# A graph layer on one core: keys, context and token mixing moved from the first stage and the prologue into the edge loop

## The chip, the cores and the metric

The kernel runs on one core of a Trainium2 chip. The metric is the time of one execution on the device in microseconds (us). The engines are PE (TensorE matmul, with PEld for its weight loads), DVE (VectorE), ACT (ScalarE), POOL (GpSimd) and SP (SyncE, which here only issues DMAs). Each has a program of its own; they meet at semaphores only.

## The reference, cut to what matters

There are N = 3125 nodes of D = 256 features (25 blocks of 128 rows, the last one short) and E = 50000 edges, sorted by destination.

```
xn = layernorm(x)
# graph attention: 4 heads of 64 features
h  = einsum('ni,hio->hno', xn, W)
e  = leaky(attn_src[:, src] + attn_dst[:, dst], 0.2) * edge_weight
p  = exp(e - max(e));  alpha = p / (segment_sum(p, dst)[dst] + 1e-10)
g  = segment_sum(h[:, src] * alpha, dst)               # per head, concatenated: 256
# linear attention over all nodes: 4 heads of 32
q, k, v = split(xn @ W_qkv);  k = softmax(k over the nodes)
context[h] = k[h].T @ v[h];   mix = (q * 32**-0.5 @ context) @ W_out + b_out
x1 = x + g + mix
# feed-forward on the better half of the tokens, 256 -> 1024 -> 256
xn2 = layernorm(x1);  w = xn2 @ wr + br
out = x1 + xn2 + (where a token ranks in the top 1561: w * (gelu(xn2 @ w1 + b1) @ w2 + b2))
```

The maximum over all edges is not known in advance: the kernel keeps a running maximum over the groups and rescales what it has accumulated.

## The kernel before, in words

All engines' programs are written out by hand; the order of the work on each engine is the order of its lines, and a `wait_ge` on a semaphore is all that couples them. There is no planner.

**First stage, blocks t = 0 to 24.** DVE takes mean and variance (L745, L787) and normalizes (`normed`, L757) into a ring of five blocks; PE transposes the block (L432); ACT copies the transposed block out of PSUM (L615); `project` on PE multiplies it by `wbig` (L417: h for 256 features, the source and destination logits, and v, 392 columns together) and by `wqk` (L423: k and q, transposed). DVE copies h out (L764, a row of the table `htab`, which SP stores with L285) and v (L765); ACT copies k and q (L604). POOL adds the output bias to x (L365). Under t = 0 DVE also makes the tables of destination indices (L806 to L828), which SP stores and reloads before the first row of `htab` goes out (L269 to L280). POOL makes the table `iotab` of block numbers at t = 20 (L363). SP loads the tokens x at the start, between the weights; the late weights (L306 to L312) and the lists of the first eight edge groups go out between the row stores.

**Prologue.** When the last row of `htab` is in memory POOL starts to gather. Meanwhile ACT exponentiates k (L623); PE transposes it (L519) and sums the context over 25 blocks (L523); DVE takes the four diagonal parts out; PE multiplies by W_out (L529); and 25 products of q with that matrix (L534) are added to x by DVE (L1034). `expand`, `turn` and `logits` for the first groups run in between.

**Edge loop, 98 groups of 512 edges.** Groups 0 to 7 are written out, groups 8 to 87 are ten passes of a hardware loop whose body holds eight groups, and 88 to 97 are written out again (`groups`, L207). For group g:
- SP loads its lists (L296 to L303); POOL gathers 4 tiles of 128 rows of `htab` by source (L383) into a ring of four groups; it may start group g + 4 when the messages of g are made.
- DVE (`step`, L1036): messages of g (L936, rows times exponentials), one-hot of g (L998), running maximum with group g + 1 (`group_max`, L930, one partition), addition of the sums of g - 1 to the accumulators (`add_last`, L941), logits of g + 2 (L911 to L923), one-hot columns of g + 3 (L870). On every second group its registers with the block numbers are loaded.
- PE (`step`, L537): the sums of g, eight matmuls of 260 columns (L483), and after the first two of them the maximum for g + 1 spread over 128 partitions (`spread`, L479); then the edge maxima of g + 2 transposed (`turn`, L472), and the destination logits of g + 3 (`expand`, L452, L460).
- ACT (`step`, L660): waits for the spread maximum, copies it twice (L666, L667), two exponentials of the logits (L671, L672), in split groups the sums of g - 1 under two masks (L658), then the rescale factors (L645, L648).

Each group's edges end in one block of nodes or in two; 24 groups are such split ones and take the branches.

**After the loop**: normalization, the second layernorm, the feed-forward over 25 blocks (L564, L577), ranks of the tokens by counting (L1126 to L1132) and the output. The change leaves it as it is but for the names of its buffers.

Of the kernel before, what the change touches and what calls it, by code (L numbers as in the profile page):

```python
# [6 lines left out]
P = 128  # L7
# [4 lines left out]
ALU = mybir.AluOpType  # L12
# [7 lines left out]
TILES = 4  # L20
RING = 4
LISTS = 8
BODY = 5


def gps_layer(nc, x_in, src_in, dst_in, ew_in, gw_in, gas_in, gad_in, wqkv_in, wout_in, bout_in,
# [25 lines left out]
    ADV = HEADS + QK  # L52
    HW = ROW + ADV
# [8 lines left out]
    LOOPS = NG // LISTS  # L62
    KSEL = max(1, int(0.5 * N))
    KK = KSEL - 1 if KSEL > 1 else 1
    assert EREST % TILES == 0 and D == HF == 256 and NB % BODY == 0 and QK == P

# [5 lines left out]
    w_d = nc.dram_tensor("w_d", (NB, P), F32, kind="Internal").ap()  # L72

    with ExitStack() as ctx:
# [10 lines left out]
        kq = sb("kq", [P, 2, NB * P])  # L85
        adv = sb("adv", [P, NB, ADV])
        wbig = sb("wbig", [P, KC, HW])
        wqk = sb("wqk", [P, KC, 2 * QK])
# [16 lines left out]
        xnT = sb("xnT", [P, BODY, KC, P])  # L105
# [35 lines left out]
        rg = sb("rg", [1, 2])  # L141
        rj = sb("rj", [1, P])
        Rsb = sb("Rsb", [P, 2])
        negR = sb("negR", [P, 2])
        Rlast = sb("Rlast", [P, NB])
# [5 lines left out]
        ksums = sb("ksums", [P, NB // BODY])  # L151
        kmaxs = sb("kmaxs", [P, NB // BODY])
        ekt = sb("ekt", [P, BODY, P])
# [13 lines left out]
        wrow = kq[:, 0, :]  # L167
        junk = kq[:, 1, :]
# [6 lines left out]
        for name in ("constants_ready y_weighted gelu_table masks_ready k_padding_zero wqkv_loaded "  # L175
                     "block_iota_ready kmax_of_batch sp_go gp_go dve_go act_go deviation_ready b_out_loaded "
                     "w_loaded late_weights_loaded a_loaded w_times_a w_a_ready stats_ready mean_var_ready "
                     "rstd_ready xn_ready xn_turned xnT_ready h_projected rows_staged attn_dst_v_taken "
                     "kq_projected kq_taken b_out_added dst_loaded table_steps tables_stored ranges_loaded "
                     "last_dst_loaded padding_loaded attn_dst_split kmax_steps k_exp ksum_steps ek_turned "  # L180
                     "ek_taken context_summed context_taken c2_multiplied c2_taken mix_multiplied mix_added "
                     "edge_max logit_sum logit_leaky logit_weighted max_turned running_max max_spread "
                     "max_copied exp_ready messages_ready columns_last columns_block attn_dst_last "
# [16 lines left out]
        FIRST_BATCHES = ((0, 1), (1, BODY - 1))  # L200
        TURN_BANKS, MIX_BANKS = (3, 4, 6), (3, 4, 6)
        WT_AT = 6
        DLP = 12

        block = ctx.enter_context(nc.Block())

# [959 lines left out]
```

## Time and profile before

| what | value |
|---|---|
| runs (3) | 829.38, 820.99, 830.68 us; median 829.38 us |
| profiled execution | 831.26 us, its span 829.2 us |
| mean granted TensorE clock | 0.841 of 2.4 GHz |
| busy share of the span | PE 84%, PEld 65%, DVE 72%, ACT 30%, POOL 56% |
| DMA | 82.60 MB, mean 100 GB/s |

The span runs from the first to the last instruction of the core. Busy shares count executing instructions; register, branch, semaphore and DMA-issuing instructions count as idle. POOL's gathers (DMA_INDIRECT) count as busy while POOL prepares them; the transfer itself runs on the DMA engines. An idle time is put down to the engine whose semaphore came last, or to "issue" where the profile shows nothing that was waited for. A matmul's duration runs to the modelled end of its result, so consecutive ones overlap: the distance of their starts is the rate.

### The profile page before, as it was taken

To read this page: it belongs to the slowest core of one execution; us is meant where nothing else is said; L and a number is where in the kernel's file an instruction comes from. 1 tells how busy PE (TensorE), PEld (TensorE's weight loads), DVE (VectorE), ACT (ScalarE), POOL (GpSimd) and SP (SyncE) were. 2 spreads that over 40 slices of the span, in tenths; PEclk is the share of its full clock that TensorE was granted. 3 is DMA by queue.
4 is the path that set the end of the run, shared out by engine and by line. 5 is a ranking of instruction groups with operands and counts; after the bars stand their busy time and mean duration, and the time that the engine had idled before them with its cause. 6 is when DMAs were issued, how large, how long until landed. Compare 5 with 4: busy or idle time off the path is not lost.

```text
span 829.2 us, 18805 instructions
## 1 busy us (share of the span) xinstructions
PE 698.8 (84%) x4369; PEld 537.4 (65%) x4370; DVE 594.7 (72%) x1631; ACT 247.1 (30%) x1013; POOL 466.6 (56%) x512
## 2 busy tenths in 40 slices
PE   3799689877878788879888888789867989999995
PEld 2577566654555565656565656566647879999994
DVE  7665267765767676766676767677769982989895
ACT  1222502222322223322232323233333422333331
POOL 5233437777777777777776777777701260333332
PEclk9999786887887878876586968787878999999998
DMA  6255415655655555655555656566400002000000
GB/s 209 58 184 79 93 53 126 142 137 133 138 131 135 134 135 136 141 128 129 129 133 125 134 135 136 126 137 138 107 21 1 1 2 80 26 33 28 26 26 22
DMA packets 104814, 82.60 MB, mean 100 GB/s; under 512 B 67133, under 2 KB 91566, under 8 KB 104561
## 3 DMA queue, kind: packets, MB, share of 16 engines
q0 software_dynamic: 18816, 52.21, 24.4%
q1 hardware_dynamic: 85873, 29.16, 16.6%
q14 instruction: 100, 0.82, 0.3%
q8 instruction: 25, 0.41, 0.2%
HBM read 74.47 MB, written 6.84 MB: 98 GB/s over the span
## 4 chain that ended last, share of the span: by engine, by line
PE 44%; issue 18%; DVE 18%; DVEq 6%; DMA 4%; ACT 3%; POOL 3%; SPq 2%; ACTq 2%; POOLq 0%
PE ps L483 17%; PE ps L564 8%; PE ps L577 8%; DVE oh L998 4%; PE ps L417 3%; POOL G L383 3%; DVEq L231 3%; PE ps L479 3%; DMA G<-htab,srcr 2%; DVE msg L936 2%; PE ps L423 2%; DVE wprod L1094 1%; DMA x<-in_x 1%; DVE G L1077 1%; ACTq L231 1%
## 5 line engine op out<-in xcount | busy, mean ns | idle before, releaser
L383 POOL DMA_INDIRECT G<-htab,srcr x392 | 372.2, 949 | 158.3 <-issue 133.5
L483 PE MATMUL ps<-msg,oh 128*128 128x260 f32 x784 | 298.6, 518 | 73.8 <-DVE oh L998 73.2
L483 PEld LDWEIGHTS ps<-msg,oh 128*128 128x128 f32 x784 | 174.1, 245 | 103.9 <-issue 78.5
L936 DVE TENSOR_TENSOR msg<-G,ps 128x1024 f32<-128x1024 f32 x98 | 119.2, 1216 | 45.1 <-issue 29.6
L564 PEld LDWEIGHTS ps<-xnT,w 128*128 128x128 f32 x800 | 98.0, 201 | 3.8 <-issue 1.8
L564 PE MATMUL ps<-xnT,w 128*128 128x128 f32 x800 | 98.5, 284 | 2.1 <-ACT wide L727 1.6
L666 ACT ACTIVATE negR<-ps 128x1 f32<-128x1 f32 x98 | 16.8, 171 | 257.8 <-PE ps L479 244.0
L577 PE MATMUL ps<-w,wide 128*128 128x256 f32 x400 | 90.4, 380 | 1.2 <-DVE acc L1101 1.2
L998 DVE TENSOR_TENSOR oh<-ps,dmr 128x512 f32<-128x512 f32 x98 | 67.3, 687 | 21.2 <-issue 19.9
L577 PEld LDWEIGHTS ps<-w,wide 128*128 128x128 f32 x400 | 74.3, 190 | 10.4 <-issue 1.4
L396 POOL TENSOR_SCALAR G<-acc,mw 128x256 f32<-128x256 f32 x25 | 23.1, 923 | 99.4 <-DVE mw L1134 90.2
L452 PE MATMUL ps<-ad,ohT 128*128 x1464 | 72.5, 175 | 5.1 <-DVE ohT L870 1.7
L452 PEld LDWEIGHTS ps<-ad,ohT 128*128 128x128 bf16 x1464 | 63.1, 118 | 9.9 <-issue 6.3
L479 PEld LDWEIGHTS ps<-rg,ones 1*128 1x128 f32 x196 | 34.7, 220 | 41.2 <-issue 41.1
L727 ACT ACTIVATE wide<-ps,b 128x128 f32<-128x128 f32 x200 | 54.2, 389 | 3.5 <-PE ps L564 3.4
L389 POOL TENSOR_TENSOR x<-x,acc 128x256 f32<-128x256 f32 x25 | 22.0, 885 | 54.5 <-DVE acc L1087 54.5
L1129 DVE TENSOR_SCALAR_CACHE_REDUCE kq<-kq,wtok 128x3125 f32<-128x3125 f32 (+24 forms) x25 | 46.6, 1866 | 0.0
L1126 DVE TENSOR_SCALAR_CACHE_REDUCE kq<-kq,wtok 128x128 f32<-128x128 f32 (+23 forms) x24 | 44.9, 1871 | 0.0
L870 DVE TENSOR_SCALAR ohT<-dstb,nodeid 128x512 bf16<-128x512 uint16 x98 | 38.6, 393 | 8.7 <-issue 7.4
L941 DVE SCALAR_TENSOR_TENSOR acc<-acc,fsc,ps 128x260 f32 x74 | 35.2, 475 | 13.2 <-issue 10.3
L417 PE MATMUL ps<-wbig,xnT 128*128 128x392 f32 x100 | 40.1, 526 | 4.3 <-DVE adv L765 4.2
L479 PE MATMUL ps<-rg,ones 1*128 1x1 f32 x196 | 43.1, 287 | 0.0
(139 smaller groups left out, 805.5 us busy)
## 6 DMA issues: line engine op xcount, KB each, us to landing
dstb<-dstu_d SPq DMA_DIRECT2D x98, 128.0 KB
G<-htab,srcr POOLq DMA_INDIRECT x392
htab<-hst SPq DMA_DIRECT2D x25, 130.0 KB, 2.6
out<-G SPq DMA_DIRECT2D x24, 128.0 KB, 1.7
x<-in_x SPq DMA_DIRECT2D x4, 640.0 KB, 8.5
w<-in_L_ffn_w SPq DMA_DIRECT2D x4, 512.0 KB
kq<-w_d SPq DMA_DIRECT2D x1, 1600.0 KB, 6.3
dmr<-dstm_d SPq DMA_DIRECT2D x98, 2.0 KB
```

The costliest lines, as they stand in the source:

```text
L383: gp.indirect_dma_start(G[:, q % RING, k, :], None, htab, bass.IndirectOffsetOnAxis(ap=srcr[:, q, k:k + 1], axis=0)).then_inc(s_g[q % RING ...
L417: m = pe.matmul(ps[:, 2 + b, 0:HW], xnT[:, t % BODY, kc, :], wbig[:, kc, :], start=(kc == 0), stop=(kc == KC - 1))
L452: m = pe.matmul(ps[:, p, 4 * k:4 * k + 4], ohT[:, columns, k:GE:TILES], ad3[:, bass.ds(b, 1), j, :].rearrange("p a h -> p (a h)"), start=F ...
L479: pe.matmul(ps[:, 5, 0:1], ones[:, :], rg[:, q % 2:q % 2 + 1], start=True, stop=True).then_inc(S["max_spread"], 1)
L483: m = pe.matmul(ps[:, 3 + p, 0:ROW], oh[:, p, k, :], msg[:, p, k, :], start=(k == 0), stop=(k == TILES - 1))
L564: m = pe.matmul(ps[:, 2 + half, (c % 4) * P:(c % 4 + 1) * P], w1[:, kc, c * P:(c + 1) * P], xnT[:, t % BODY, kc, :], start=(kc == 0), stop ...
L577: m = pe.matmul(ps[:, 4 + t % 3, 0:D], hT[:, t % 2, c, :], w2[:, c, :], start=(c == 0), stop=(c == FC - 1))
L727: m = act.activation(hT[:, t % 2, c, :], ps[:, 2 + half, (c % 4) * P:(c % 4 + 1) * P], ACT.Gelu_apprx_tanh, bias=b1[:, c:c + 1])
L936: dve.tensor_tensor(msg[:, p, :, 0:HF].rearrange("p k (h o) -> p k h o", h=HEADS), G[:, q % RING, :, 0:HF].rearrange("p k (h o) -> p k h o ...
L998: dve.tensor_tensor(oh[:, q % 2, :, :], iotap.unsqueeze(1).to_broadcast([P, TILES, P]), dmr[:, q, :].unsqueeze(2).to_broadcast([P, TILES, ...
L1126: dve.tensor_scalar(junk[:, 0:lo], wrow[:, 0:lo], wt, 0.0, ALU.is_ge, ALU.add, accum_out=cnt[:, t, 0:1]).then_inc(S["counted"], 1)
L1129: dve.tensor_scalar(junk[:, lo:N], wrow[:, lo:N], wt, 0.0, ALU.is_gt, ALU.add, accum_out=cnt[:, t, 1:2]).then_inc(S["counted"], 1)
```

## The change

- The first stage projects h and the two attention logits only (264 columns); `evacuate_h` moves from DVE to ACT. The transposed blocks `xnT` of all 25 blocks are kept, instead of a ring of five.
- Block 0 is loaded, normalized and projected by itself. The other token loads, and b_out's, move from SP's queue to ACT's, ahead of ACT's first activation. The index tables are stored after row store 6 instead of before the first. Three edge lists go out among the last row stores, five after them, then the late weights. POOL zeroes acc block by block behind the bias addition, instead of in one piece at the start.
- Keys: PE makes k for 512 nodes at a time (`keys`, seven chunks, two of them ahead of the first `expand`); DVE takes them out together with their maximum.
- The running maximum: `turn` becomes a product of the edge maxima, broadcast over 128 columns, with the identity, so that DVE's `group_max` leaves the negated maximum on all 128 partitions. `spread`, its place inside the sums, and ACT's two copies go.
- The ten passes of the loop are split in five and five. In the first five, each of the five groups in SLOTS takes one node block: ACT stages the transposed block and the exponential of its keys (`stage_keys`), PE makes v and the transposed keys (`make_pair`, at the end of its step) and adds the pair of the slot before to the context; ACT takes the pair out of PSUM in the following group, after that group's exponentials and before its rescaling. Between the halves the context, W_out and the transposed W_q are multiplied into one 256x256 matrix M (`take_context`, `multiply_context`). In the last five passes PE multiplies a staged block by M (`mix`) and DVE adds the product to x in the following group (`add_mix`).

```diff
+SLOTS = (0, 2, 3, 5, 6)
...
-    HW = ROW + ADV
+    HW = ROW + HEADS
...
+        def looped(eng, lo, hi, step, side=None):
+
+            with eng.Fori(lo, hi):
+                for q in range(LISTS):
+                    step(None, q, side)
...
+                    if t == TABLES_AT:
+                        store_tables()
+                    if t == TABLES_AT + 7:
+                        spread_tables()
+                    if t == TABLES_AT + 10:
+                        sp.wait_ge(S["tables_stored"], 80)
+                    if t in LISTS_AT:
+                        step(LISTS_AT.index(t), LISTS_AT.index(t))
+                unrolled(step, range(len(LISTS_AT), LISTS))
+                for tile, array in loads:
+                    sp.dma_start(tile, array).then_inc(S["late_weights_loaded"], 16)
+                looped(sp, 1, LOOPS - 1, step)
+                unrolled(step, TAIL)
...
+                gp.memset(acc[:, t, :], 0.0).then_inc(S["acc_zeroed"], 1)
...
-                if t >= 2:
-                    pe.wait_ge(S["kq_taken"], t - 1)
-                for c in range(2):
-                    for kc in range(KC):
-                        m = pe.matmul(ps[:, 4 + b, c * P:(c + 1) * P], wqk[:, kc, (1 - c) * P:(2 - c) * P], xnT[:, t % BODY, kc, :],
-                                      start=(kc == 0), stop=(kc == KC - 1))
-                m.then_inc(S["kq_projected"], 1)
...
+            def keys(c):
+
+                lo = 4 * c
+                if c == 0:
+                    pe.wait_ge(S["wqkv_loaded"], 32)
+                if c >= 2:
+                    pe.wait_ge(S["k_taken"], c - 1)
+                wide = min(WIDE, N - c * WIDE)
+                for kc in range(KC):
+                    nodes = xnT[:, lo:lo + 4, kc, :] if wide == WIDE else xnT[:, lo, kc, 0:wide]
+                    m = pe.matmul(ps[:, 5 + c % 2, 0:wide], wqkv[:, kc, QK:2 * QK], nodes, start=(kc == 0), stop=(kc == KC - 1))
+                m.then_inc(S["k_projected"], 1)
 
...
-                pe.transpose(ps[0:1, 2, 0:P], rm[:, q % 2:q % 2 + 1], ident[:, :]).then_inc(S["max_turned"], 1)
-
-            def spread(q, ready):
-
-                pe.wait_ge(S["running_max"], ready)
-                if ready is n:
-                    pe.wait_ge(S["exp_ready"], n)
-                pe.matmul(ps[:, 5, 0:1], ones[:, :], rg[:, q % 2:q % 2 + 1], start=True, stop=True).then_inc(S["max_spread"], 1)
-
-            def add_messages(p, tiles=range(TILES)):
...
+            def add_context(s, last=False):
+                return pe.matmul(ps[:, 6, 0:P], pair[:, s, 0:P], pair[:, s, P:2 * P], start=False, stop=last, skip_group_check=True)
+
+            def make_pair(q):
+
+                if q in SLOTS:
+                    pe.wait_ge(S["pair_taken"], passed)
+                    pe.wait_ge(S["block_staged"], passed)
+                    pe.sem_inc(S["pe_go"], 1)
+                    add_context((SLOTS.index(q) - 1) % BODY)
+                    for kc in range(KC):
+                        pe.matmul(ps[:, 5, 0:P], xs[:, kc, :], wqkv[:, kc, 2 * QK:3 * QK], start=(kc == 0), stop=(kc == KC - 1))
+                    pe.transpose(ps[:, 5, P:2 * P], es[:, :], ident[:, :]).then_inc(S["pair_made"], 1)
+                    pe.reg_add(passed, passed, 1)
+
+            def multiply_context():
+                pe.wait_ge(S["pair_taken"], NB + 1)
+                add_context(BODY - 1, True).then_inc(S["context_summed"], 1)
+                pe.wait_ge(S["context_taken"], MIX_HEADS)
+                pe.wait_ge(S["late_weights_loaded"], 16 * 9)
+                pe.matmul(ps[:, 6, 0:D], ctxT[:, :], wout[:, :], start=True, stop=True).then_inc(S["c2_multiplied"], 1)
+                pe.wait_ge(S["c2_taken"], 1)
+                for kc in range(KC):
+                    m = pe.matmul(ps[:, 5, kc * D:(kc + 1) * D], wqT[:, kc, :], C2[:, :], start=True, stop=True)
+                m.then_inc(S["m_multiplied"], 1)
+                pe.wait_ge(S["m_taken"], 1)
+
+            def mix(q):
+                if q in SLOTS:
+                    pe.wait_ge(S["mix_added"], passed)
+                    pe.wait_ge(S["block_staged"], passed)
+                    pe.sem_inc(S["pe_go"], 1)
+                    for kc in range(KC):
+                        m = pe.matmul(ps[:, 5, 0:D], xs[:, kc, :], M[:, kc, :], start=(kc == 0), stop=(kc == KC - 1))
+                    m.then_inc(S["mix_multiplied"], 1)
+                    pe.reg_add(passed, passed, 1)
+
+            def step(g, q, side=None):
+                sums(q)
                 if q % 2 == 1 and (g is None or g + 3 < NG):
                     load_ranges(pe, regs, cursor, (q + 3) % LISTS)
                 if g is None or g + 2 < NG:
                     turn(q + 2, n)
                 if g is None or g + 3 < NG:
                     expand((q + 3) % LISTS, n)
...
+            unrolled(step, FIRST)
+            pe.wait_ge(S["query_taken"], 1)
+            looped(pe, 1, 1 + TURNS, step, make_pair)
+            multiply_context()
+            looped(pe, 1 + TURNS, LOOPS - 1, step, mix)
+            pe.wait_ge(S["mix_added"], 2 * NB + 1)
...
+            for i, (base, blocks) in enumerate(NORMED[1:]):
+                if i < len(NORMED) - 2:
+                    act.dma_start(x[:, base:base + blocks, :], x_in[base * P:(base + blocks) * P, :].rearrange("(b p) c -> p b c", p=P)).then_inc(s_x[1 + i], 16)
+                else:
+                    act.dma_start(x[:, base:NB - 1, :], x_in[base * P:(NB - 1) * P, :].rearrange("(b p) c -> p b c", p=P)).then_inc(s_x[1 + i], 16)
+                    act.wait_ge(S["constants_ready"], 1)
+                    act.dma_start(x[0:REST, NB - 1, :], x_in[(NB - 1) * P:N, :]).then_inc(s_x[1 + i], 16)
+                if i == 0:
+                    act.wait_ge(S["constants_ready"], 8)
+                    act.activation(negR[:, 0:1], eps[:, 0:1], ACT.Sqrt)
+            act.dma_start(boutb[:, :], bout_in.rearrange("(a d) -> a d", a=1).to_broadcast([P, D])).then_inc(S["b_out_loaded"], 16)
...
+            def evacuate_h(t):
+
+                act.wait_ge(S["h_projected"], t + 1)
+                if t >= BODY:
+                    act.wait_ge(s_tab[t % BODY], 16 * (t // BODY))
+                act.activation(hst[:, t % BODY, :], ps[:, 2 + t % 2, 0:ROW], ACT.Copy).then_inc(S["rows_staged"], 1)
+                act.activation(adst[:, t, :], ps[:, 2 + t % 2, ROW:HW], ACT.Copy).then_inc(S["attn_dst_taken"], 1)
...
+            def stage_tokens(done):
+                act.activation(xs[:, :, :], xnT[:, bass.ds(act.snap(u, min_val=0, max_val=NB - 1), 1), :, :].rearrange("p a c n -> p (a c) n"), ACT.Copy).then_inc(S[done], 1)
+
+            def stage_keys(q):
+
+                if q - 1 in SLOTS:
+                    act.wait_ge(S["pair_made"], made)
+                    act.activation(pair[:, SLOTS.index(q - 1), :], ps[:, 5, 0:2 * P], ACT.Copy).then_inc(S["pair_taken"], 1)
+                    act.reg_add(made, made, 1)
+                if q in SLOTS:
+                    stage_tokens("tokens_staged")
+                    t = act.snap(u, min_val=0, max_val=NB - 1)
+                    act.activation(es[:, :], kT[:, bass.ds(t * P, P)], ACT.Exp, bias=kmax[:, 1:2], accum_out=ksums[:, bass.ds(t, 1)]).then_inc(S["block_staged"], 1)
+                    act.reg_add(u, u, 1)
+
+            def stage_block(q):
+
+                if q in SLOTS:
+                    act.wait_ge(S["mix_multiplied"], made)
+                    act.sem_inc(S["act_go"], 1)
+                    stage_tokens("block_staged")
+                    act.reg_add(u, u, 1)
+                    act.reg_add(made, made, 1)
+
...
+            def step(g, q, side=None):
                 p = q % 2
                 if q % 2 == 0:
                     load_ranges(act, regs, cursor, q)
                 first, start, last = blocks_of(act, regs, q)
-                act.wait_ge(S["max_spread"], n)
-                act.activation(negR[:, p:p + 1], ps[:, 5, 0:1], ACT.Copy, scale=-1.0).then_inc(S["max_copied"], 1)
-                act.activation(Rsb[:, p:p + 1], ps[:, 5, 0:1], ACT.Copy).then_inc(S["max_copied"], 1)
+                act.wait_ge(S["running_max"], n3)
                 act.wait_ge(S["summed_last"], n3)
-                act.wait_ge(S["max_copied"], copies)
                 e = et[:, p, 0:16].rearrange("p (k h) -> p k h", k=TILES)
                 act.activation(msg[:, p, :, HF:ROW], e, ACT.Exp, bias=negR[:, p:p + 1])
                 act.activation(exq[:, p, :, :], e, ACT.Exp, bias=negR[:, p:p + 1]).then_inc(S["exp_ready"], 1)
+                if side:
+                    side(q)
                 act.wait_ge(S["added_last"], n)
                 act.wait_ge(S["max_kept_last"], n)
...
+                before = -LOWEST if ready == 3 else negR[:, (q + 1) % 2:(q + 1) % 2 + 1]
+                dve.tensor_scalar(rj[:, :], ps[:, 2, 0:P], -1.0, before, ALU.mult, ALU.min, accum_out=negR[:, q % 2:q % 2 + 1]).then_inc(S["running_max"], 1)
...
+            for c in range(CHUNKS):
+                lo, hi = c * WIDE, min((c + 1) * WIDE, N)
+                dve.wait_ge(S["k_projected"], c + 1)
...
+            def take_context():
+                dve.wait_ge(S["block_staged"], NB)
+                dve.tensor_reduce(ksum[:, 0:1], ksums[:, :], AX.X, ALU.add).then_inc(S["ksum_steps"], 1)
+                dve.wait_ge(S["ksum_steps"], 1)
+                dve.reciprocal(ksum[:, 1:2], ksum[:, 0:1]).then_inc(S["ksum_steps"], 1)
+                dve.wait_ge(S["context_summed"], 1)
+                for h in range(MIX_HEADS):
+                    s = slice(h * DIM_HEAD, (h + 1) * DIM_HEAD)
+                    dve.tensor_copy(ctxT[s, s], ps[s, 6, s]).then_inc(S["context_taken"], 1)
+                dve.wait_ge(S["c2_multiplied"], 1)
+                dve.wait_ge(S["ksum_steps"], 2)
+                dve.tensor_scalar(C2[:, :], ps[:, 6, 0:D], ksum[:, 1:2], float(DIM_HEAD) ** -0.5, ALU.mult, ALU.mult).then_inc(S["c2_taken"], 1)
+
+            def add_mix(q):
+                if q - 1 in SLOTS:
+                    t = dve.snap(u, min_val=0, max_val=NB - 1)
+                    a = x[:, bass.ds(t, 1), :].rearrange("p a c -> p (a c)")
+                    dve.wait_ge(S["mix_multiplied"], mixed)
+                    dve.sem_inc(S["dve_go"], 1)
+                    dve.tensor_tensor(a, ps[:, 5, 0:D], a, ALU.add).then_inc(S["mix_added"], 1)
+                    dve.reg_add(u, u, 1)
+                    dve.reg_add(mixed, mixed, 1)
+
...
+                if side:
+                    side(q)
```

## Rows read from the trace of the kernel before

**Rows 1.** The chain that ended last, from the page: shares of the span by engine.

```profile
PE 44%; issue 18%; DVE 18%; DVEq 6%; DMA 4%; ACT 3%; POOL 3%; SPq 2%; ACTq 2%; POOLq 0%
```

**Rows 2.** Stretches: length, busy us (x instructions) per engine, clock, DMA share, GB/s.

```profile
50.00:100.00 50.00, 42.02 (x255) 33.45 (x254) 23.08 (x66) 17.88 (x53) 18.64 (x17) 0.90 0.45 93
...
200.00:300.00 100.00, 82.78 (x511) 56.64 (x510) 69.03 (x197) 26.89 (x129) 75.17 (x79) 0.78 0.59 135
```

**Rows 3.** Groups by line: xcount | busy, mean ns | idle before, releasers.

```profile
L383 POOL DMA_INDIRECT G<-htab,srcr x392 | 372.2, 949 | 158.3 <-issue 133.5 <-DVE msg L936 24.8
...
L936 DVE TENSOR_TENSOR msg<-G,ps 128x1024 f32<-128x1024 f32 x98 | 119.2, 1216 | 45.1 <-issue 29.6 <-ACT ps L672 15.0
```

**Rows 4.** Lines L383 and L936: ns min/median/max, first and last start us.

```profile
L383 POOL DMA_INDIRECT G<-htab,srcr x392: 940/946/1194, 92.5 to 602.1; - x196
...
L936 DVE TENSOR_TENSOR msg<-G,ps x98: 1201/1221/1223, 123.1 to 613.1; 128x1024 f32<-128x1024 f32 x98
```

**Rows 5.** DVE timeline (start us, us, instruction, [idle, releaser]): messages opening groups 8 to 88.

```profile
159.90 1.22 DVE L936 TENSOR_TENSOR msg<-G,ps 128x1024 f32<-128x1024 f32 x1 [0.17 <-ACT ps L672]
...
202.76 1.22 DVE L936 TENSOR_TENSOR msg<-G,ps 128x1024 f32<-128x1024 f32 x1 [3.60 <-issue]
...
230.24 1.21 DVE L936 TENSOR_TENSOR msg<-G,ps 128x1024 f32<-128x1024 f32 x1
...
234.20 1.21 DVE L936 TENSOR_TENSOR msg<-G,ps 128x1024 f32<-128x1024 f32 x1
...
569.40 1.22 DVE L936 TENSOR_TENSOR msg<-G,ps 128x1024 f32<-128x1024 f32 x1
```

**Rows 6.** Timeline of POOL: the seventeenth gather.

```profile
125.13 0.94 POOL L383 DMA_INDIRECT G<-htab,srcr  x1 [12.75 <-DVE msg L936]
```

**Rows 7.** Timeline of one block of the first stage, PE.

```profile
78.74 0.38 PE L432 MATMUL ps<-ident,xn 128*128 128x128 f32 x2
...
78.96 1.48 PE L417 MATMUL ps<-wbig,xnT 128*128 128x392 f32 x4
...
80.28 1.05 PE L423 MATMUL ps<-xnT,wqk 128*128 128x128 f32 x8
```

**Rows 8.** Groups by line and shape: xcount | busy, mean ns | idle before.

```profile
L1034 DVE TENSOR_TENSOR x<-ps,x 128x256 f32<-128x256 f32 x25 | 10.6, 425 | 3.9 <-PE ps L534 3.8
...
L604 ACT ACTIVATE kq<-ps 128x256 f32<-128x256 f32 x25 | 9.6, 383 | 47.2 <-PE ps L423 47.2
```

**Rows 9.** Timeline around POOL's table of block numbers.

```profile
60.38 5.54 POOL L363 TENSOR_TENSOR wide<-iota,blkbase 128x3200 f32<-128x3200 f32 x1
61.58 4.48 DVE L757 TENSOR_SCALAR xn<-x,mv,rstd 128x256 f32<-128x256 f32 x1
...
67.10 0.72 POOL L365 TENSOR_TENSOR x<-x,boutb 128x256 f32<-128x256 f32 x1 [0.23 <-DVE xn L757]
```

**Rows 10.** Timeline of the start: two token loads; PE's restart.

```profile
9.86 3.63 SPq L246 DMA_DIRECT2D x<-in_x  x2
...
26.11 2.95 PE L417 MATMUL ps<-wbig,xnT 128*128 128x392 f32 x4 [4.17 <-DVE adv L765]
```

**Rows 11.** Timeline of the prologue: DVE's first one-hot columns.

```profile
91.19 0.35 DVE L870 TENSOR_SCALAR ohT<-dstb,nodeid 128x512 bf16<-128x512 uint16 x1 [4.16 <-issue]
```

**Rows 12.** Timeline of a group in the loop, PE at full clock.

```profile
460.52 0.68 PE L483 MATMUL ps<-msg,oh 128*128 128x260 f32 x2 [0.62 <-DVE oh L998]
...
461.43 1.58 PE L483 MATMUL ps<-msg,oh 128*128 128x260 f32 x6
...
462.08 0.26 ACT L672 ACTIVATE ps<-et,negR 128x16 f32<-128x16 f32 x1
...
463.27 0.20 ACT L648 ACTIVATE Rlast<-Rsb 128x1 f32 x1
...
463.29 0.73 PE L452 MATMUL ps<-ad,ohT 128*128 x12
```

**Rows 13.** Timeline of a group in the loop, PE at half clock: its last six sums.

```profile
410.28 2.97 PE L483 MATMUL ps<-msg,oh 128*128 128x260 f32 x6
```

More of the change, by code:

```diff
@@ L72, in gps_layer @@
     w_d = nc.dram_tensor("w_d", (NB, P), F32, kind="Internal").ap()
+    NORMED = ((0, 1), (1, BODY - 1)) + tuple((lo, BODY) for lo in range(BODY, NB, BODY))
     with ExitStack() as ctx:
@@ L200, in gps_layer, with unrolled @@
         FIRST_BATCHES = ((0, 1), (1, BODY - 1))
[L201 removed]
         WT_AT = 6
         DLP = 12
+        TABLES_AT, LISTS_AT = 6, (17, 19, 21)
         block = ctx.enter_context(nc.Block())
[L207 to L218 removed]
+        FIRST, TAIL = range(LISTS), range((LOOPS - 1) * LISTS, NG)
+        def looped(eng, lo, hi, step, side=None):
+            with eng.Fori(lo, hi):
+                for q in range(LISTS):
+                    step(None, q, side)
+        def unrolled(step, which):
+            for g in which:
+                step(g, g % LISTS)
         numbers = iter(range(1000))
@@ L436, in _ @@
             project(NB - 1)
+            keys(0)
+            keys(1)
             pe.wait_ge(S["ranges_loaded"], 32)
@@ L524, in _ @@
-            spread(0, 3)
+            expand(1, 2)
+            for c in range(2, CHUNKS):
+                keys(c)
+            pe.wait_ge(S["k_taken"], CHUNKS)
+            for kc in range(KC):
+                m = pe.transpose(ps[:, 5, kc * P:(kc + 1) * P], wqkv[:, kc, 0:QK], ident[:, :])
+            m.then_inc(S["query_turned"], 1)
+            pe.matmul(ps[:, 6, 0:P], zrow[:, 0:P], zrow[:, 0:P], start=True, stop=False, skip_group_check=True)
+            turn(0, 2)
             turn(1, 3)
@@ L535, in _ @@
-            pe.wait_ge(S["mix_added"], NB)
-            def step(g, q):
-                sums(q, lambda: spread(q + 1, n) if g is None or g + 1 < NG else None)
+            def add_context(s, last=False):
[10 more added lines that the diff above has]
+                    pe.reg_add(passed, passed, 1)
@@ L691, in step @@
                 rescale(fsc, p, last, "factor_last", n5, "max_kept_last")
-                for r, by in ((n, 1), (n3, 1), (n5, 1), (copies, 2)):
-                    act.reg_add(r, r, by)
+                for r in (n, n3, n5):
+                    act.reg_add(r, r, 1)
             act.wait_ge(S["masks_ready"], 2)
             act.wait_ge(S["iota_taken"], 1)
-            groups(step)(act)
+            unrolled(step, FIRST)
+            act.wait_ge(S["kmax_steps"], 2)
+            act.wait_ge(S["k_padding_set"], 1)
+            looped(act, 1, 1 + TURNS, step, stage_keys)
+            act.wait_ge(S["m_multiplied"], 1)
+            act.activation(M[:, :, :], ps[:, 5, 0:KC * D].rearrange("p (c n) -> p c n", c=KC), ACT.Copy).then_inc(S["m_taken"], 1)
+            act.reg_mov(u, 0)
+            act.reg_mov(made, 1)
+            looped(act, 1 + TURNS, LOOPS - 1, step, stage_block)
+            unrolled(step, TAIL)
             act.wait_ge(S["added_last"], n)
@@ L778, in _ @@
             m.then_inc(S["w_a_ready"], 1)
-            invert(0, BODY, 1)
-            for t in range(BODY):
+            invert(1, BODY - 1, 2)
+            for t in range(1, BODY):
                 normed(t).then_inc(S["xn_ready"], 1)
@@ L1037, in step @@
+            def step(g, q, side=None):
                 add, leak, weight, reduce = [lambda: None] * 4
```

300 lines of the change are left out of this document (110 added, 190 removed).

## The prediction

> **What bounds the kernel now.** I read the chain of waits first, then the stretches, then the two groups that recur in every edge group, then the order of time. The chain [rows 1] names PE for 44% and DVE for 18%, but that averages over stages. The stretches [rows 2] separate them: in 50 to 100 us (mostly projection) PE has 42.0 of 50 us; in the edge loop (200 to 300) PE has 82.8, POOL 75.2 and DVE 69.0 of 100, at a granted clock of 0.78, so PE moves between its two levels. No engine is full there, so the rate has to be read from the groups.
>
> The groups give it [rows 3]: 392 gathers of 949 ns with 133.5 us of "issue" idle between them, about 0.3 each, are 1.25 us apiece, 5.0 per edge group, 40.0 for a pass of eight. DVE's messages multiply runs once per group, from 123.1 to 613.1 [rows 4], so its starts are the clock of the loop: 159.90 (group 8) to 569.40 (group 88) [rows 5] are ten passes in 409.5 us, 40.95 each. But POOL also waited 24.8 us for DVE's messages [rows 3], 12.75 of it at once, with all four ring slots full while DVE was still in the prologue [rows 6]; later, too, DVE is now and then the late one. So **two limits lie within 1 us of each other**: POOL at 40.0, and the chain of DVE, PE and ACT. What lengthens that chain costs in full; shortening it gains at most 0.95 us a pass.
>
> Once per pass DVE also sits 3.6 us ahead of its messages with no releaser but "issue" [rows 5]; ten such idles make 29.6 us [rows 3]. They come at the loop's jump back; the change keeps the number of passes, so they stay. What follows the last messages (613.1 to 829.2, 216 us) it leaves alone.
>
> **The change, part by part.** *Projection.* A block's PE work is 0.22 us of transposes, then 1.32 of four 392-column matmuls (78.96 to 80.28), then eight products for k and q in 1.05, of which the next block overlaps 0.17 [rows 7]: 2.42 with no gap. The eight go; 392 columns become 264, so 1.32 becomes 0.89, and PE needs 1.1. ACT takes over the copies out of PSUM: 0.38 for a 256-column one [rows 8], two such and a short one, about 1.0. POOL's bias addition takes 0.72 and alternates with DVE's normalization 0.23 apart where pressed [rows 9], 0.95; POOL now also zeroes a block of acc each time, which I put at 0.3, between nothing and another 0.72, since it reads nothing. So 1.3 us a block, bounds 1.1 and 1.7.
>
> Here a row speaks against the change: beside POOL's 5.54 us table of block numbers one normalization took 4.48 us [rows 9]. PE at 2.42 a block hid that; at 1.3 I charge 3 us of it. The Trainium skill (SBUF — State Buffer, section "SBUF: two separate sides") says that DVE and GpSimd share a port pair under an exclusive lock, the loser blocking for the whole instruction. The trace agrees with that; taken strictly, the zeroing would cost its full length in every block.
>
> The start: PE restarted at 26.11, after DVE's index tables and copies, with two blocks done [rows 10]. Afterwards five normalized blocks are ahead of the tables and DVE no longer copies, so five are done by then. But the token loads move to ACT's queue; SP spent 3.63 us issuing two of them [rows 10], and ACT's first square root stands behind all of its issues, to about 11 us. That moves the restart to 27.5 (bounds 26 and 31). Then 20.5 blocks by 1.3, plus 3: the projection ends near 57. On SP's queue the table stores move behind row store 6, four issues and a wait that held back every row until now; the first three edge lists stand between the last row stores and cost about a microsecond. The late weights move behind the lists; their first use is after the fifth pass, which hides them.
>
> *Prologue.* Register loads held DVE 4.16 us before its first one-hot [rows 11]; that stays, with about 2 us of splitting ahead of it and 3 of two expansions behind. New on the path are seven key chunks, each four 512-column matmuls: by the 392-column row 1.7 us at full clock, twice that after an idle stretch; five lie behind the expansions, 10 us. Their copies on DVE run beside the next chunk; without that cover they would add about 0.8 each. Logits, maximum and exponential: 5. First messages near 81, **42 us earlier** (36 to 47). The context chain and the 25 mixing products leave this stretch. The gathers start near 61 instead of 92.5 [rows 4] and fill the ring by 81, so the 12.75 us stall goes.
>
> *Every group.* The `spread` matmul leaves PE (it holds the third sum to 461.43, 0.91 after the first) [rows 12] and two copies leave ACT; the maximum becomes a two-pass product, +0.1. DVE's wait for ACT's exponential goes: 15.0 us over 98 groups [rows 3], 1.2 per eight.
>
> *First five passes: keys and context.* PE gets, five times a pass, seven products of 128 columns: by the row of eight [rows 7] 0.95 at full clock, 1.6 to 1.9 at half. A PE step at full clock ends 3.5 us after its first sum (460.52 to 464.02) [rows 12]; without the spread and with the second pass 3.05, so a pair is ready 4.15 after its group's sums begin. **The price is a new wait on ACT:** one step later ACT waits for that pair before it rescales, and the exponential of the group after that is queued behind. From the pair on: copy 0.38 [rows 8]; rescale 0.8 (1.1 from 462.34 to 463.47 [rows 12], partly overlapped); on even groups a register load, 1.75 (two cost DVE 4.16, so under 2.1); exponentials 0.4: 3.3. Where the next block is staged, 0.8 more. DVE starts its messages 2 us before PE's sums and needs 3.96 a step (230.24 to 234.20) [rows 5], 4.5 with a register load, so it is ready for group 2 at 6.5, and the exponential comes at 4.15 + 3.3 = 7.45: 1.0 late. The same working gives 2.0 at group 4 (staging and load), 0.9 at group 7, nothing elsewhere: 3.9. A pass: 40.95 − 1.2 + 3.9 = 43.7. At half clock six sums take 2.97 instead of 1.58 [rows 12, 13] and the pair comes about 2.5 later; I put 0.3 a pass on that: **44.0**.
>
> *Last five passes: mixing.* DVE adds 0.43 [rows 8] and a wait, five times: 2.5. PE's four 256-column products take about 1.0, and only behind neighbouring slots does ACT still come late, 0.75. 40.95 − 1.2 + 3.25 = **43.0**. Between the halves the fused matrix makes four hops over PE, DVE and ACT with a PSUM copy on each: 4 us.
>
> *Sum*, on the profiled span of 829.2: −42 (head), −1.2 (first eight groups), 5 · 3.05 + 5 · 2.05 = +25.5 (passes), +4 (between), −1.5 (last ten groups): −15.2, **814**. The execution itself took 831.3, 2.1 more than its span; the median of the runs is 829.4, equal to the span, so 814 stands for the median too.
>
> **The rivals.** *A. Forecast, 814, chance 0.42.* The head gains 42 and the passes give back over half. On its own terms 802 to 828.
>
> *B. The passes stay with POOL.* If ACT's wait falls into slack, the gathers set the rate: they start 31.5 earlier, lose no 12.5, and 3 us of later stalls go: 829.2 − 47 = 782. For it: 1.25 us a gather, and ACT busy for 27 of 100 us [rows 2]. Against: POOL was already waiting for DVE. Chance 0.2.
>
> *C. Slower: PE at its half level becomes the bound of the passes.* A half-clock step is 3.05 + 1.9 = 4.95, plus 1.6 in five of eight: 48 a pass. The head's gain is spent when a pass reaches 45.0; 2% slower needs 46.7. At 48.3: 829.2 − 40.7 + 73 − 4 = 857. For it: clock 0.78 with PE at 83% [rows 2], and PE's net work a pass grows by 3 us (full) to 6 (half). Against: 0.90 where PE was packed [rows 2]. Chance 0.18.
>
> *D. PE rises to 2.4 GHz in the passes.* With fewer gaps the clock goes to 1.0 and the half-clock part of the 40.95, about 1.2, falls away: passes of 42.5 and 42.0, so 829.2 − 40.7 + 13 = 802. The Trainium skill (TensorE: Matmul & The Clock Gate, Part 1) states that idleness throttles the array and activity releases it; by that rule the added products partly pay for themselves. [rows 2] lean that way, 0.90 against 0.78, but the two stretches differ in more than that. Chance 0.2.
>
> **How the numbers follow.** The likeliest is 814. The range 780 to 846 takes in B at the low end, the head's bounds and passes up to 47; the outer part of C is left out. A measurement of this kernel can tell about 2% from no change, 812.8 to 846.0. Faster: B, most of D, a third of A, 0.48; slower: most of C and a corner of A, 0.15; same: 0.37.
>
> **What would show it.** Right: first messages near 81; gathers from 61 with no stall at the fifth group; in passes one to five the messages of groups 2, 4 and 7 waiting for ACT's exponential; 44 and 43 us a pass, and POOL waiting for messages in more groups than now. B would show passes of 40.0 and DVE waiting for G, C a clock below 0.75 and PE without idle, D a clock above 0.9. The forecast fails at its root if the projection stays above 1.7 us a block, for then the head gives less than 30, or if ACT never waits for the pair.

## The result, and the profile after

The changed kernel takes **834.8 us** (833.8 to 837.6 over 4 runs), the kernel before 829.2: a ratio of 1.0086, with a 95% interval of 1.0043 to 1.0128. It is slightly slower, where 814 and faster had been forecast. The profiled span went from 829.2 to 831.8.

The first view is again the line of DVE's messages, which open every edge group, beside that of the gathers, by groups (busy, mean ns | idle before, releasers).

```profile
L389 POOL DMA_INDIRECT G<-htab,srcr x392 | 373.1, 952 | 171.8 <-issue 122.8 <-DVE msg L985 48.9
L985 DVE TENSOR_TENSOR msg<-G,ps 128x1024 f32<-128x1024 f32 x98 | 119.0, 1214 | 73.4 <-ACT ps L726 52.1 <-issue 20.9
```

The messages' line by itself (ns min/median/max, first and last start):

```profile
L985 DVE TENSOR_TENSOR msg<-G,ps x98: 1200/1217/1223, 92.2 to 617.9; 128x1024 f32<-128x1024 f32 x98
```

Against [rows 3, 4]: the first messages come 30.9 us earlier (92.2, was 123.1), the last 4.8 later. DVE's wait for ACT's exponential (L726) went from 15.0 to 52.1 us, and POOL's wait for messages doubled, 24.8 to 48.9. Some 9 us of the 52.1 stand where "issue" stood before (29.6, now 20.9); all idle time ahead of the messages rose from 45.1 to 73.4. So the loop is longer, and DVE waits for ACT more, POOL for DVE. Cut by the starts of groups 0, 8, 48, 88 and 97 (us; "rest" is the span less the last start):

| profile | first messages | first 8 groups | passes 1-5 | passes 6-10 | groups 88 to 97 | rest | span |
|---|---|---|---|---|---|---|---|
| before | 123.1 | 36.8 | 203.7 | 205.8 | 43.7 | 216.1 | 829.2 |
| after | 92.2 | 36.8 | 234.8 | 215.7 | 38.4 | 213.9 | 831.8 |
| predicted difference | -42 | -1.2 | +15.2 | +14.3 | -1.5 | 0 | -15.2 |
| measured difference | -30.9 | -0.1 | +31.2 | +9.9 | -5.3 | -2.2 | +2.6 |

(The 4 us between the halves are put to passes 6 to 10 in the prediction's row; in the trace they fall into pass 5, which took 51.4.)

*The wait in the passes.* Pass 3, timelines of ACT, DVE and PE (start, us, instruction, [idle, releaser]): group 24's messages, sums and pair, the sums of group 25, the messages, sums and pair of group 26, and the messages of group 28.

```profile
219.89 1.22 DVE L985 TENSOR_TENSOR msg<-G,ps 128x1024 f32<-128x1024 f32 x1 [3.60 <-issue]
...
223.34 3.38 PE L490 MATMUL ps<-msg,oh 128*128 128x260 f32 x8 [5.59 <-DVE oh L1047]
...
228.15 0.27 PE L536 MATMUL ps<-ident,es 128*128 128x128 f32 x1
228.26 1.92 PE L490 MATMUL ps<-msg,oh 128*128 128x260 f32 x8
...
228.46 0.38 ACT L700 ACTIVATE pair<-ps 128x256 f32<-128x256 f32 x1 [4.49 <-PE ps L536]
229.47 0.29 ACT L678 ACTIVATE fsc<-negRlast,negR 128x1 f32 x1 [0.63 <-issue]
229.88 0.20 ACT L681 ACTIVATE negRlast<-negR 128x1 f32 x1
231.73 0.31 ACT L725 ACTIVATE msg<-et,negR 128x16 f32<-128x16 f32 x1 [1.64 <-issue]
231.94 0.26 ACT L726 ACTIVATE ps<-et,negR 128x16 f32<-128x16 f32 x1
...
232.23 1.22 DVE L985 TENSOR_TENSOR msg<-G,ps 128x1024 f32<-128x1024 f32 x1 [2.20 <-ACT ps L726]
...
234.20 3.81 PE L490 MATMUL ps<-msg,oh 128*128 128x260 f32 x8 [2.80 <-DVE oh L1047]
...
240.08 0.27 PE L536 MATMUL ps<-ident,es 128*128 128x128 f32 x1
240.39 0.38 ACT L700 ACTIVATE pair<-ps 128x256 f32<-128x256 f32 x1 [5.56 <-PE ps L536]
...
244.18 1.22 DVE L985 TENSOR_TENSOR msg<-G,ps 128x1024 f32<-128x1024 f32 x1 [3.33 <-ACT ps L726]
```

ACT sits idle 4.49 us until PE has turned the staged keys (L536); then come the copy, the rescaling, a register load (the 1.64 of "issue") and the exponential, and DVE's messages for group 26 are 2.20 late, for group 28 3.33. PE waits for DVE in its turn. The sums of group 24 follow 5.59 us of idle, most of it DVE's stop at the loop's jump back (group 24's messages, at 219.89, stand behind 3.60 us of "issue", as once a pass in the kernel before [rows 5]); they take 3.38 us at a granted clock of 0.56, where the sums of group 25 take 1.92 at 1.00. The late messages of group 26 then leave PE idle for 2.80 us, and its sums take 3.81 us at 0.50, the lower of the two levels.

*The head.* ACT's queue at the start; then ACT's and SP's when the stage is under way.

```profile
3.53 2.68 ACTq L633 DMA_DIRECT2D x<-in_x  x1
6.25 4.79 ACTq L635 DMA_DIRECT2D x<-in_x  x1
11.07 6.85 ACTq L639 DMA_DIRECT2D boutb<-in_L_mix_b_out  x1
17.97 0.29 ACT L643 ACTIVATE sd<-mv,eps 128x1 f32<-128x1 f32 x1 [15.22 <-issue]
...
33.25 0.44 PE L445 MATMUL ps<-ident,xn 128*128 128x128 f32 x2 [2.70 <-DVE xn L823]
...
45.04 1.06 PE L424 MATMUL ps<-wbig,xnT 128*128 128x264 f32 x4
45.93 0.38 PE L445 MATMUL ps<-ident,xn 128*128 128x128 f32 x2
46.15 1.06 PE L424 MATMUL ps<-wbig,xnT 128*128 128x264 f32 x4
...
44.93 0.39 SPq L269 DMA_DIRECT2D dstm_d<-wide  x1
45.37 9.26 SPq L283 DMA_DIRECT2D htab<-hst  x7
...
53.09 0.39 ACT L650 ACTIVATE hst<-ps 128x260 f32<-128x260 f32 x1 [4.01 <-DMA htab<-hst]
```

Three issues hold ACT for 14.3 us, so its first square root runs at 17.97 and PE restarts at 33.25 (26.11 before [rows 10]). A block then takes 1.11 us (45.04 to 46.15; 2.42 before [rows 7]), until ACT waits 4.01 us for the row stores that queue behind the index tables.

### The profile page after: what moved, and what is told of

It is laid out like the page before. It is cut to its first block, busy times and chain, and to the rows that moved or that the text cites. A ratio compares the mean times of both kernels' runs of the same rounds, so it can differ in the third digit from the quotient of the medians.

```text
span 831.8 us, 18655 instructions
## 1 busy us (share of the span) xinstructions
PE 653.5 (79%) x4258; PEld 541.0 (65%) x4259; DVE 574.4 (69%) x1591; ACT 253.8 (31%) x936; POOL 469.0 (56%) x537
## 4 chain that ended last, share of the span: by engine, by line
PE 42%; issue 20%; DVE 16%; ACTq 6%; DVEq 5%; ACT 5%; DMA 3%; POOL 2%; SPq 0%; POOLq 0%
PE ps L490 14%; PE ps L596 8%; PE ps L609 7%; DVE oh L1047 3%; PE ps L465 3%; ACTq L239 2%; POOL G L389 2%; PE ps L424 2%; DVEq L239 2%; PE ps L486 2%; PE ps L557 2%; DVE wprod L1164 1%; DMA G<-htab,srcr 1%; DVE stats L811 1%; DVE G L1147 1%
## 5 line engine op out<-in xcount | busy, mean ns | idle before, releaser
L490 PE MATMUL ps<-msg,oh 128*128 128x260 f32 x784 | 250.0, 474 | 98.7 <-DVE oh L1047 98.2
L985 DVE TENSOR_TENSOR msg<-G,ps 128x1024 f32<-128x1024 f32 x98 | 119.0, 1214 | 73.4 <-ACT ps L726 52.1
L465 PE MATMUL ps<-ad,ohT 128*128 x1464 | 77.4, 176 | 3.0 <-DVE ohT L919 2.0
L465 PEld LDWEIGHTS ps<-ad,ohT 128*128 128x128 bf16 x1464 | 67.3, 118 | 9.5 <-issue 3.4
L725 ACT ACTIVATE msg<-et,negR 128x16 f32<-128x16 f32 x98 | 30.1, 308 | 137.7 <-DVE rj L979 85.4
L486 PEld LDWEIGHTS ps<-ident,rm 128*128 128x128 f32 x196 | 40.6, 225 | 37.6 <-DVE rm L972 30.8
L486 PE MATMUL ps<-ident,rm 128*128 128x128 f32 x196 | 47.0, 326 | 16.7 <-DVE rm L972 16.2
L1199 DVE TENSOR_SCALAR_CACHE_REDUCE xnT<-kT,wtok 128x3125 f32<-128x3125 f32 (+24 forms) x25 | 46.6, 1865 | 0.0
L1196 DVE TENSOR_SCALAR_CACHE_REDUCE xnT<-kT,wtok 128x128 f32<-128x128 f32 (+23 forms) x24 | 44.9, 1871 | 0.0
L777 ACT ACTIVATE xnT<-ps 128x256 f32<-128x256 f32 x25 | 9.6, 384 | 109.1 <-PE ps L586 109.1
L919 DVE TENSOR_SCALAR ohT<-dstb,nodeid 128x512 bf16<-128x512 uint16 x98 | 36.8, 375 | 6.6 <-issue 5.3
L678 ACT ACTIVATE fsc<-negRlast,negR 128x1 f32 x98 | 28.8, 294 | 40.9 <-issue 26.4
## 6 DMA issues: line engine op xcount, KB each, us to landing
x<-in_x ACTq DMA_DIRECT2D x3, 640.0 KB, 11.3
```

Of the source, the lines that this page charges most:

```text
L465: m = pe.matmul(ps[:, p, 4 * k:4 * k + 4], ohT[:, columns, k:GE:TILES], ad3[:, bass.ds(b, 1), j, :].rearrange("p a h -> p (a h)"), start=F ...
L486: pe.matmul(ps[:, 2, 0:P], rm[:, q % 2:q % 2 + 1].to_broadcast([P, P]), ident[:, :], start=True, stop=True).then_inc(S["max_turned"], 1)
L490: m = pe.matmul(ps[:, 3 + p, 0:ROW], oh[:, p, k, :], msg[:, p, k, :], start=(k == 0), stop=(k == TILES - 1))
L919: dve.tensor_scalar(ohT[:, 0, :], dstb[:, q, :], nodeid[:, bass.ds(last, 1)], None, ALU.is_equal).then_inc(S["columns_last"], 1)
L985: dve.tensor_tensor(msg[:, p, :, 0:HF].rearrange("p k (h o) -> p k h o", h=HEADS), G[:, q % RING, :, 0:HF].rearrange("p k (h o) -> p k h o ...
L1196: dve.tensor_scalar(junk[:, 0:lo], wrow[:, 0:lo], wt, 0.0, ALU.is_ge, ALU.add, accum_out=cnt[:, t, 0:1]).then_inc(S["counted"], 1)
```

## The experiments

Each run's ratio is to the kernel before, on the same chip.

**1. l_late: ACT handles the pair last in its step.**

```diff
                 act.activation(exq[:, p, :, :], e, ACT.Exp, ...)
-                if side:
-                    side(q)
...
                 rescale(fsc, p, last, "factor_last", n5, "max_kept_last")
+                if side:
+                    side(q)
```

> ACT handles the pair (and stages the next block) at the end of its step, behind the rescaling, in both halves. Theory 2 (the exponential stands behind ACT's wait for the pair): passes one to five fall from 46 to 42 to 44 us, DVE's messages no longer wait 2.2 and 3.3 us at groups 2 and 4, the whole 10 to 20 us shorter. Rival (PE's added products set the pace of the passes, at half clock above all): passes stay at 45 to 47, the whole within 4 us.

Measured: **795.6 us**, ratio 0.9615 [0.9569, 0.9661]; passes 210.1 and 202.5, 38 us less in all. The same instructions run in a shorter time: the ten passes after, then in this kernel (length; busy (x) of PE, its loads, DVE, ACT, POOL; clock; DMA share; GB/s).

```profile
128.93:363.77 234.84, 176.13 (x1195) 142.77 (x1194) 141.91 (x420) 71.83 (x279) 156.78 (x165) 0.81 0.52 121
363.77:579.48 215.71, 173.35 (x1178) 136.68 (x1178) 154.62 (x454) 66.71 (x245) 151.97 (x160) 0.86 0.55 125
```

```profile
126.39:336.50 210.11, 166.05 (x1195) 133.26 (x1194) 141.69 (x420) 71.81 (x281) 157.53 (x166) 0.88 0.58 135
336.50:539.02 202.52, 172.20 (x1178) 136.74 (x1178) 154.38 (x454) 66.52 (x244) 150.08 (x158) 0.85 0.58 133
```

ACT is busy for 71.8 us in the first half of both, yet one takes 24.7 us less. DVE's wait for ACT fell to 10.4 us in all, and 1.0 a pass is left at group 2 of the first half:

```profile
L985 DVE TENSOR_TENSOR msg<-G,ps 128x1024 f32<-128x1024 f32 x98 | 118.9, 1214 | 37.0 <-issue 26.4 <-ACT ps L726 10.4
```

Nothing was taken out, only the order on one engine changed. The gain was twice the upper end of my expectation: 24.7 us came from the first half, which I had priced, and 13.2 from the second, which had lost to the wait too.

**2. l_bare: no keys, context or mixing work in the passes** (`looped` without its last argument on PE, ACT and DVE).

> Leaves out all keys, context and mixing work in the ten passes (PE, ACT and DVE alike); the rest of the edge loop is that of the changed kernel. It measures the bare pass. Prediction's working: 39.8 to 40.0, POOL's gathers the limit, so ten passes in 400 against 450.6. Rival (something other than the added work made the loop slower, such as the two-pass product for the maximum or code loading): passes stay above 42.

Measured: 793.9 us, 0.9611 [0.956, 0.9663]; passes 208.0 and 199.9, 40.8 each. The rival (above 42) is ruled out. All the added work costs 4.8 us over ten passes once ACT's order is right (l_late less this), and 42.7 in the order of the change. This kernel still makes the matrix between the halves, which falls into its pass 5 (44.1 us); its other nine passes take 40.4 each, the same nine before 41.05. So the expected 39.8 to 40.0 was too low by about 0.5, and taking the spread away gained about 0.6 a pass. DVE's wait for ACT ahead of the messages of these passes fell from 9.1 to 3.8 us (all of it at group 48), but its wait for gathered rows rose from 5.0 to 12.4: the gathers took up much of the gain.

**3. l_products: PE's products alone.**

```diff
-                    pe.wait_ge(S["pair_taken"], passed)
-                    pe.wait_ge(S["block_staged"], passed)
...
-            looped(act, 1, 1 + TURNS, step, stage_keys)
+            looped(act, 1, 1 + TURNS, step)
```

(and likewise in the mixing half, where DVE's additions go too; the buffers that PE reads hold zeros)

> PE does all added products of the ten passes (on zeros), but nothing waits for them: ACT stages and copies nothing, DVE adds nothing. Theory 2 (ACT's wait): passes within 1.5 us of the bare ones. Rival (PE's work itself): passes one to five at 44 to 47, near those of the changed kernel.

Measured: 791.0 us, 0.9561 [0.9516, 0.9606]; passes 209.1 and 203.0. The two windows of passes one to five, bare and with the products:

```profile
128.34:336.32 207.98, 155.11 (x1021) 119.25 (x1019) 141.14 (x420) 45.65 (x181) 156.85 (x165) 0.82 0.60 136
```

```profile
127.70:336.77 209.07, 166.28 (x1195) 132.63 (x1193) 141.20 (x420) 45.65 (x181) 157.58 (x166) 0.88 0.58 136
```

PE works 11.2 us more and the stretch is 1.1 longer; the mean granted clock rose from 0.82 to 0.88. PE's added work is not what the passes pay for.

**4. l_first: PE makes the pair earlier.**

```diff
                 sums(q)
+                if side:
+                    side(q)
...
                     expand((q + 3) % LISTS, n)
-                if side:
-                    side(q)
```

> PE makes the pair (and the mixing product) right behind its sums, ahead of the turn of the maximum and the expansion; ACT stays as in the changed kernel. Theory 2 (the wait for the pair holds the exponential): the pair comes 1.5 to 2.5 us earlier, the waits at groups 2, 4 and 7 shrink by as much from 2.3, 2.9 and 1.2, passes one to five fall to 42 to 44, the whole 10 to 25 us shorter than the changed kernel's 834.8. Rival (ACT's own added copies, 1.4 us a staged block ahead of its rescaling, are the cost, and the wait only hides them): passes stay above 45; or the delayed turn becomes the new wait and passes rise.

Measured: 812.2 us, 0.9804 [0.976, 0.9848]; passes 216.5 and 209.0, or 43.3 and 41.8. ACT kept its order and its copies; only the pair came sooner, and 25 of the 38 us came back. Of DVE's waits in passes one to five, those at group 2 fell from 2.0 us (mean of five) to 0.4, at group 4 from 2.3 to 0.5, at group 7 from 1.2 to 0. The other 13 us are the second half of the rival: the turn of the maximum now stands behind the pair, and DVE's wait for it (L979) rose from 4.8 to 20.7 us over the ten passes (3.3 in l_late). So the cost goes with the lateness of the pair; ACT's copies, which kept their place, show no share of their own.

**5. after_three, before_three: three gathers a group instead of four** (`range(TILES - 1)` from group 4 on, in the changed kernel and in that of before).

> The changed kernel with three gathers an edge group. Theory 2 (its passes are bound by the chain through ACT's wait, POOL only waits for messages): passes one to five within 1.5 us of 46.9, six to ten within 1.5 of 43.1. Rival (gathers take part in the longer passes): 3 us or more less.

> The kernel before with three gathers an edge group instead of four, from group 4 on (the fourth tile keeps old rows): POOL's share of a pass falls from 40.0 to 30.0 us. The prediction's reading (two limits within 1 us of each other): passes stay at 39.5 to 41. Rival (gathers alone bound the passes): 37 us or less.

Measured, one run each: after_three 830.8 us, passes 232.9 and 215.5, 2.2 us less in all; before_three 819.0, passes 196.5 and 205.0, 40.1 each, 8.0 us less in all. The gathers had next to no part in the longer passes. In the kernel before the two limits did lie within 1 us, though 5.8 of the 8.0 us fell in its first pass (42.9 to 37.1).

**6. h_tokens: ACT issues only the blocks 1 to 9.**

```diff
-            for i, (base, blocks) in enumerate(NORMED[1:]):
-                ...
-            act.dma_start(boutb[:, :], ...)
+            load_tokens(act, 1)
+            ...
+            load_tokens(act, 2)
...
                 sp.dma_start(avec[:, which, :], ...)
+                load_tokens(sp, 3)
+                sp.dma_start(boutb[:, :], ...)
                 sp.dma_start(dl[0:NG - 1, :], ...)
                 ...
+                for i in range(4, len(NORMED)):
+                    load_tokens(sp, i)
```

> ACT issues only the token blocks 1 to 9; the other loads and b_out go to SP's queue, ahead of the index tables. Theory 1 (ACT's own DMA issues, 2.68, 4.79 and 6.85 us, hold its first square root until 17.97): square root near 5 to 8 us, restart after the tables at 23 to 27 instead of 33.25, first messages 6 to 10 us earlier than 92.18, the whole 6 to 10 us shorter. Rival (the loads themselves land that late, whoever issues them, or SP's table stores follow behind): the square root moves but the restart stays within 2 us and the time within 2 us.

Measured: 822.6 us, 0.9936 [0.9903, 0.9969]. ACT's first square root:

```profile
4.11 0.29 ACT L650 ACTIVATE sd<-mv,eps 128x1 f32<-128x1 f32 x1 [1.36 <-DVE mv L821]
```

PE restarts at 23.94 instead of 33.25, the first messages come at 84.3, 7.9 us earlier, the span is 7.8 shorter (by the medians 12.2, more than expected).

**7. h_tables: the index tables behind row store 2.**

```diff
-        TABLES_AT, LISTS_AT = 6, (17, 19, 21)
+        TABLES_AT, LISTS_AT = 2, (17, 19, 21)
```

> The index tables are stored behind row store 2 instead of 6 (their reload and its wait move with them), nothing else. Theory 3 (the table stores fill the DMA engines just when PE runs at full rate, and the row stores, five buffers deep, hold ACT 4.0 us near 50): that stall goes, first messages 2.5 to 4 us earlier than 92.18. Rival (the stores fall on other row stores instead): first messages within 1 us of 92.18.

Measured: 829.2 us, 1.0004 [0.998, 1.0028], 5.6 us less than the change by the medians. ACT's 4.01 us wait is gone, the first stage ends 5.2 us earlier (62.41, was 67.62), the first messages come at 85.6: 6.5 us earlier, more than the 2.5 to 4 expected. The rest of that gain lies in the key chunks behind the expansions; why they came closer I did not test.

**8. The repairs together.** late_tokens is 1 with 6; late_tokens_tables is 1 with 6 and 7; three_gathers is the last with three gathers.

> Both: ACT handles the pair behind its rescaling, and issues only the token blocks 1 to 9. If the two losses are independent, their gains add: first messages near 82 to 84, passes near 41, 785 to 790 us in all (795.6 less 8). Rival (an earlier start is given back to the gathers, which at 1.25 us apiece then bound the passes): 792 or more.

> The same with the tables stored behind row store 2: 2 to 4 us less again, 782 to 787, if theory 3 holds; the same as without it, if the stall moves.

> The version with all three repairs, with three gathers an edge group. If gathers bound its passes (40.2 to 42), they fall to 37 to 39.5 and the time by 10 to 30 us; if the chain of DVE, PE and ACT has the same length, nothing moves.

Measured: late_tokens **786.8 us**, 0.9511 [0.9475, 0.9546]; late_tokens_tables **783.1 us**, 0.9455 [0.9425, 0.9485], both faster than both kernels, the second by 46 us against the kernel before. The token loads took another 8.8 us off l_late's 795.6, close to the 7.8 that experiment 6 took off the span. Whether the tables add to that is not settled: the medians are 3.6 us apart but the intervals overlap, and the profiles can't tell. In them the first messages came 3.4 us earlier (76.5 against 79.8) and the passes took 6.7 longer (419.7 against 413.0), but the profiled execution with the tables took 787.3 us, 4.1 above its median. three_gathers took 769.6 us in one run, passes 205.0 and 197.3, 40.2 each: neither 37 to 39.5 nor unmoved. Without a quarter of the gathers 13.5 us go by the median (the kernel before, in one run beside it, was 4.0 faster too), 17.4 in the passes of the profiles. So the gathers seem to bind the passes of this version in part, and behind them stands a chain of about 40 us; it is one run.

## Why the prediction was wrong

It missed the span by 17.8 us (831.8 against 814): +11.1 in the head, +1.1 in the first eight groups, +11.6 in the passes and between, -3.8 from group 88 to 97, -2.2 in the rest. The mechanism of the loss (the head gains, ACT's wait for the pair takes it back) was named, but two terms were mis-sized: the head's gain of 42 us, which came to 30.9, and the wait on ACT of 3.9 a pass with 0.3 for half clock, which came to 5.8.

**The head, "42 us earlier (36 to 47)".** 30.9 came, outside the bounds. Two terms failed. "ACT's first square root stands behind all of its issues, to about 11 us": I priced the issues by SP's 3.63 us for two [rows 10], but six token loads and b_out took ACT to 17.97, and the restart came at 33.25, not 27.5: 5.75 us. Experiment 6 shows that the issues counted. The Trainium skill (DMA: Bandwidth & Descriptors, section "Issuing engines are not separate DMA queues") calls the sequencer's time for starting a DMA usually small beside the DMA itself. Here the trace differs: b_out's issue held ACT for 6.85 us, of 14.5 until the data had landed. The second term is SP's queue: I saw the table stores move behind row store 6 and credited it as a hindrance removed; they then stood in front of the row stores that the stage at 1.1 us a block needed. From restart to the end of the stage 34.4 us passed instead of 29.5; with the tables moved (experiment 7) it was 28.4 for 21 blocks, 1.35 each. So the 1.3 us a block came out, with the bounds, but in part by luck: in a steady run PE sets the pace at 1.11, and the rest is its wait for blocks at the restart. The 3 us for POOL's table were not paid: three normalizations took 6.36 us beside it, but PE had blocks in hand and did not stop. The prologue took 24.6 us, 24 predicted.

**The wait on ACT, "3.9 a pass".** It came at groups 2, 4 and 7, as worked out, with means of 2.0, 2.3 and 1.2 us in passes one to five: 5.8 in all with the small rest. (The 1.3 at group 0 is no new loss; with the "issue" beside it that idle is 2.7 a pass, in the kernel before 2.6.) The step that failed is "a pair is ready 4.15 after its group's sums begin" and "I put 0.3 a pass" on half clock. In the rows above the pair of group 24 is ready 5.1 us after (223.34 to 228.42), that of group 26 6.1 (234.20 to 240.35), because their sums follow an idle stretch of PE and run mostly or wholly at half clock. ACT's way from the pair to the exponential took 3.8 us at group 26, not 3.3. The first idle stretch is that of the jump back, which I had left out of the pair's price; the second is the wait's own doing: a late exponential stops DVE, DVE stops PE, and PE's next pair is later still. That chain is read from this stretch; no run takes the clock out of it alone. The Trainium skill (TensorE: Matmul & The Clock Gate, Part 1) has idleness as the cause of the low level. The trace agrees here: 0.56 and 0.50 over sums behind 5.59 and 2.80 us of idle, 1.00 over sums with PE busy before them. The sum had a slip as well: the terms it shows make group 4 come 1.8 late and group 7 about nothing, 2.8 a pass and not 3.9, so naming group 7 owed something to luck.

**The mixing half, "43.0".** 215.7 us is 43.1, right for a wrong reason: DVE's additions, put at 2.5 a pass, cost almost nothing (passes of 40.5 in l_late, which has them, 40.0 in l_bare), and the wait for ACT, put at 0.75, was 2.4 at groups 4 and 7.

**The pass without the wait, 39.75.** Bare it is 40.4, without the pass that holds the matrix between the halves. The spread's 1.2 us came to about 0.6: in the passes DVE's wait for ACT had been 9.1 us, 0.9 a pass, and the gathers' 40.0 stood just behind (DVE's wait for gathered rows rose, experiment 2). Put right, the first half adds up: 44.0 and 1.6 for the wait and 0.65 here are 46.2 a pass, where 46.0 was measured without pass 5's extra.

**Between the halves, 4 us:** pass 5 took 51.4, 4.9 more than the three before it; right. **The last groups** went faster by 5.3 instead of 1.5: 38.4 us for the nine steps from group 88 to 97, 4.27 each, within DVE's 3.96 to 4.5. Why stays open; fewer gathers alone did not do it in the kernel before (43.3 in before_three, 43.7 with all). The 2.2 us behind the last messages stay open too.

**The rivals.** B (passes with POOL) is ruled out by after_three. C (PE's half level as the bound) is ruled out by l_products and l_late, which have the same products in passes of 42 us or less; its clock effect is in, as a part of the wait. D (added work raises the clock and pays for itself) describes l_products: 0.88 instead of 0.82. In the change itself the first half stood at 0.81, as in the kernel before.

## What to carry to other kernels

Work that was hung onto this loop cost by its place in an engine's order more than by its duration (42.7 us or 4.8 for the same instructions): a wait for another engine belongs behind everything that the next step needs from this one. When pricing such a wait, price its feedback too: here the engine that it starved ran its next work at half clock. An engine that computes early should issue no more DMAs than it needs first, and a transfer moved out of the way of one stage has to be looked for in front of the next.

## What the runs showed of the hardware that was not expected

A DMA issue held ACT for up to 6.85 us (three of them 14.3) while the token loads were in flight (a median of 11.3 us to landing), and SP for 5.50. Filling PE's gaps was nearly free: 11.2 us of added products lengthened five passes by 1.1, with the mean granted clock at 0.88 instead of 0.82.
